# First layer: head norm's scale and shift folded to the queries, sums of squares moved, row maxima half a group ahead

## The reference

```python
q = (layernorm(x, ln_q_g, ln_q_b) @ Wq + bq).reshape(b, c, HEAD, HD)      # 16 heads of 16
k, v = ...                                                                # the same from Wkv
q, k = apply_rotary(q * scale, x), apply_rotary(k * scale, x)             # scaled by the norm of x's rows
qn, kn = layernorm(q, ln_h_g, ln_h_b), layernorm(k, ln_h_g, ln_h_b)       # over a head's 16 features
att = softmax(einsum(qn, kn) / sqrt(HD))                                  # 1024 queries x 1024 keys
a = einsum(att, v) @ Wo + bo
```

## Time and profile before

| | |
|---|---|
| median of three runs | 2325.57 us (2319.04 to 2331.56) |
| profiled execution | 2323.5 us, its span 2322.0 us |
| busy over the span | TensorE 2008.8, VectorE 1449.2, ScalarE 1252.5, POOL 876.0 us |
| projection, first normalisation to last evacuation | about 32 to 205 us |
| attention, first row score to last output | 205.3 to 629.3 us |
| granted TensorE clock, 61 to 70 us, 70 to 79 us | 0.51, 1.00 of 2.4 GHz |

### The profile page before, as it was taken

One profiled execution on the slowest core, in us unless ns is written; L12 is line 12 of the kernel. 1 busy time (PEld: TensorE's weight loads), 2 busy tenths in 40 slices (PEclk: granted clock), 3 DMA queues, 4 the chain that ended last, 5 costly groups with the idle time before them and its releaser, 6 DMA issues. The chain is left out here.

```text
span 2322.0 us, 41383 instructions
## 1 busy us (share of the span) xinstructions
PE 2008.8 (87%) x11710; PEld 1336.4 (58%) x11710; DVE 1449.2 (62%) x3073; ACT 1252.5 (54%) x2550; POOL 876.0 (38%) x899
## 2 busy tenths in 40 slices
PE   4886999999767769999738899999788999997698
PEld 1442233333144559999714577777544777775587
DVE  4776888888055669999447665665255555543443
ACT  0573577777733337777214477777144777771322
POOL 1221000000035547798153177777100666670100
PEclk7895799999977879999869999999898999998899
DMA  7953000000061148899421011212000011112000
GB/s 212 289 95 46 11 1 0 0 0 1 25 183 78 69 138 262 264 281 278 139 68 50 8 44 42 50 44 53 19 0 1 24 23 32 23 35 68 0 19 18
DMA packets 186850, 173.82 MB, mean 75 GB/s; under 512 B 20755, under 2 KB 171653, under 8 KB 185734
## 3 DMA queue, kind: packets, MB, share of 16 engines
q1 hardware_dynamic: 174662, 143.23, 22.3%
q0 software_dynamic: 10720, 29.44, 3.8%
q10 hardware_dynamic: 1376, 0.02, 0.0%
HBM read 96.15 MB, written 61.60 MB: 68 GB/s over the span
## 5 line engine op out<-in xcount | busy, mean ns | idle before, releaser
L2611 POOL TENSOR_TENSOR w_rest<-work,w_head 128x512 fp32r<-128x512 f32 (+3 forms) x384 | 395.3, 1042 | 223.5 <-ACT w_head L2568 221.1
L769 DVE TENSOR_REDUCE half_max<-m_ps 128x1 f32<-128x512 f32 x512 | 316.6, 682 | 53.7 <-PE m_ps L694 53.2
L2457 DVE TENSOR_REDUCE piece_max<-m_ps 128x1 f32<-128x512 f32 (+3 forms) x384 | 200.8, 548 | 203.4 <-PE m_ps L2384 159.9
L823 ACT ACTIVATE weights<-s_ps 128x512 f32<-128x512 f32 x512 | 266.4, 602 | 100.1 <-PE s_ps L709 100.1
L2564 ACT ACTIVATE work<-s_ps 128x512 f32<-128x512 f32 (+3 forms) x384 | 187.6, 488 | 100.9 <-PE s_ps L2412 96.0
L2568 ACT ACTIVATE w_head<-work 128x512 fp32r<-128x512 f32 (+3 forms) x384 | 201.4, 524 | 57.0 <-PE o_ps L2421 46.0
L694 PE MATMUL m_ps<-kT,qT 96*128 (+1 forms) x512 | 211.8, 416 | 6.5 <-DVE half_max L769 4.5
L709 PE MATMUL s_ps<-qT,kT 99*128 (+1 forms) x512 | 191.3, 386 | 7.3 <-ACT weights L823 7.3
L2421 PE MATMUL o_ps<-w_head,lat_head 128*128 128x512 f32 (+3 forms) x384 | 184.3, 480 | 1.6 <-POOL w_rest L2611 1.5
L859 POOL COPY v_now<-v 128x83 f32 (+1 forms) x64 | 16.1, 258 | 375.3 <-PE o_ps L721 370.0
L709 PEld LDWEIGHTS s_ps<-qT,kT 99*128 (+1 forms) x512 | 49.0, 98 | 160.7 <-ACT weights L823 66.8
(11 more groups left out here) (393 smaller groups left out, 5038.6 us busy)
## 6 DMA issues: line engine op xcount, KB each, us to landing
slots<-zero SPq DMA_DIRECT2D x8, 3456.0 KB, 27.4
rows<-slots SPq DMA_DIRECT2D x64, 256.0 KB, 3.4
slots<-ex_out SPq DMA_DIRECT2D x64, 256.0 KB, 3.0
ex_wgv<-in_L_ffn_wg_dram SPq DMA_DIRECT2D x72, 176.0 KB, 3.0
ex_wgv<-in_L_ffn_wv_dram SPq DMA_DIRECT2D x72, 176.0 KB, 3.2
ex_wo<-in_L_ffn_wo_dram SPq DMA_DIRECT2D x72, 128.0 KB, 3.1
oT<-work SPq DMA_DIRECT2D x64, 128.0 KB
w_down<-l_inverse SPq DMA_DIRECT2D x32, 256.0 KB
```

The source lines that it names most:

```text
L769: dve.tensor_reduce(half_max[:, u:u + 1], m_ps[:, BANK[u], :], AX.X, ALU.max).then_inc(max_done, 1)
L823: act.activation(w[:, s % 2 * 4 + j, :], s_ps[:, BANK[4 * s + j], :], ACT.Exp, scale=HD ** -0.5).then_inc(w_done, 1)
L2457: dve.tensor_reduce(piece_max[:, qt, k0 // 512:k0 // 512 + 1], m_ps[:, r % 2, 0:n], AX.X, ALU.max).then_inc(d["max_done"], 1)
L2611: pool.tensor_tensor(w_rest[:, s % 3, c0:512], w[:, s % 3, c0:512], w_head[:, s % 3, c0:512], ALU.subtract).then_inc(d["w_rest_done"], 1)
```

## The change

The product of the two normalised heads, (yq g + b)(yk g + b) summed over the features, differs from (yq g² + g b) yk only by terms that are the same for all keys of a query, and the softmax drops those. So the queries are multiplied by g² and g b is added, and the keys stay as they are: L441 and L444 act on half of the columns, and two small products at the start make g² and g b.

In the projection's steps VectorE sums the squares of tile t before it centres tile t+1 (`variance`), and ScalarE takes the deviation after the first two of the four evacuations, with the copy, the squares and the other two behind it.

In the attention the row scores are ordered by halves of the queries: the first 32 of a group belong to the first 512 queries of all four heads. The maxima are split, turned, copied and placed twice per group, each half for itself, and the lead is 11 steps (half a group and three) instead of 19. Four transposes of 12 columns take the place of one of 96, the copy is 12 x 512 instead of 96 x 128, and one transfer takes the place of three.

```diff
-        v_ones = m.sem("pr_v_ones")
+        v_ones, both_done = m.sem("pr_v_ones"), m.sem("pr_both_done")
...
+                dve.tensor_tensor(b_h[:, :], g_h[:, :], b_h[:, :], ALU.mult).then_inc(both_done, 1)
+                dve.wait_ge(both_done, 1)
+                dve.tensor_tensor(g_h[:, :], g_h[:, :], g_h[:, :], ALU.mult).then_inc(both_done, 1)
+                dve.wait_ge(both_done, 2)
...
-                def scale(t, u):
+                def variance(t, u):
 
                     dve.wait_ge(sq_done, t + 1)
                     dve.tensor_reduce(hvar[:, u, :], oth[:, u], AX.X, ALU.add).then_inc(sqs_done, 1)
+
+                def scale(t, u):
+
...
-                    dve.tensor_tensor(own[:, u], val[:, u], g_h[:, :].unsqueeze(1).to_broadcast([P, NH, HD]), ALU.mult
+                    dve.tensor_tensor(own[:, u, 0:H0, :], val[:, u, 0:H0, :],
+                                      g_h[:, :].unsqueeze(1).to_broadcast([P, H0, HD]), ALU.mult
                                       ).then_inc(unit_done, 1)
                     dve.wait_ge(unit_done, 2 * t + 2)
-                    dve.tensor_tensor(val[:, u], own[:, u], b_h[:, :].unsqueeze(1).to_broadcast([P, NH, HD]), ALU.add
+                    dve.tensor_tensor(val[:, u, 0:H0, :], own[:, u, 0:H0, :],
+                                      b_h[:, :].unsqueeze(1).to_broadcast([P, H0, HD]), ALU.add
                                       ).then_inc(val_done, 1)
 
                 def step(t, u, b):
                     more = not isinstance(t, int) or t + 1 < T
                     if more:
                         rotate_parts(t + 1, 1 - u, (t + 1) // TB if b is None else b)
+                    variance(t, u)
                     if more:
                         centre(t + 1, 1 - u)
                     scale(t, u)
...
-                        evacuate(before, t - 2, u)
+                        evacuate(before, t - 2, u, range(2))
+                    deviation(t, u)
                     if not isinstance(t, int) or t > 0:
                         more_parts(t - 1, 1 - u)
                     if more:
                         squares(t + 1, 1 - u)
-                    deviation(t, u)
+                    if not isinstance(t, int) or t > 1:
+                        evacuate(before, t - 2, u, range(2, 4))
...
-    LEAD = 3
+    HALF = NU // 2
+    LEAD = 8 + 3
...
-            return [(1 + more, u) if 1 + more <= left else None for more, u in ahead]
+            return [(more, u) if more <= left else None for more, u in ahead]
...
-                    j, qt, kh = u // 16, u // 2 % 8, u % 2
+                    j, qt, kh = u % HALF // 8, u // HALF * 4 + u // 2 % 4, u % 2
...
-                    pe.transpose(t_bf[0:QK0, 0:P], shift[:, :, :], c.identb[:, :]).then_inc(shT_done, 1)
+                    for q in range(4):
+                        i = pe.transpose(t_bf[0:SHIFT_ROWS, q * P:(q + 1) * P],
+                                         shift[:, q].rearrange("p i j -> p (i j)"), c.identb[:, :])
+                    i.then_inc(shT_done, 1)
...
-                    if u == 0:
-                        pe.wait_ge(placed, g * PLACED + PLACED)
+                    if kt == 0 and j == 0:
+                        pe.wait_ge(placed, g * 2 * PLACED + (qh + 1) * PLACED)
...
-                        turn_outputs(g, 0, False)
+                        turn_outputs(g, 0, True)
+                    if s == 5:
+                        turn_shift(g, 1)
                     if s == 13 and left:
-                        turn_shift(g + 1)
+                        turn_shift(g + 1, 0)
...
-                for u in range(NU):
+                for u in range(4 * LEAD):
+                    if u == HALF + 3:
+                        turn_shift(0, 0)
                     row_scores(0, u)
-                for u in range(4 * LEAD):
-                    if u == 3:
-                        turn_shift(0)
-                    row_scores(1, u)
...
+                    if s == 4:
+                        parts(g, 1)
                     if s == 12 and left:
-                        parts(g + 1)
+                        parts(g + 1, 0)
...
+                        if s == 6 and j == 0:
+                            copy_shift(g, 1)
                         if s == 14 and j == 0 and left:
-                            copy_shift(g + 1)
+                            copy_shift(g + 1, 0)
...
-                for g in range(NG):
-                    sp.wait_ge(sh_copied, g + 1)
-                    for part in range(3):
-                        row = QK0 + part
-                        sp.dma_start(q_g[row:row + 1, g, :, :].rearrange("o h (t n) -> o (h t) n", n=P),
-                                     shift_rows[32 * part:32 * part + 32, :]).then_inc(placed, 16)
+                for n in range(2 * NG):
+                    sp.wait_ge(sh_copied, n + 1)
+                    first = n % 2 * 512
+                    sp.dma_start(q_g[QK0:ROWS0, n // 2, :, first:first + 512], shift_rows[0:SHIFT_ROWS, :]
+                                 ).then_inc(placed, 16)
```

More of the change, by code:

```diff
@@ L524, in more_parts, with evacuate @@
                     act.activation(stack[:, u, :, 4 * HD:5 * HD], rest[:, :, :], ACT.Copy).then_inc(p2_done, 1)
-                def evacuate(b, t, u):
-                    for i in range(4):
+                def evacuate(b, t, u, banks=range(4)):
+                    for i in banks:
                         act.wait_ge(turned, t * 4 + (i + 1))
@@ L638, in l0_attend @@
         half_max = l.sb("half_max", [P, NU])
[L639 to L642, removed]
+        row_max = l.sb("row_max", [P, HALF // 2])
+        rest = l.sb("max_rest", [P, HALF // 2])
+        shift = l.sb("max_parts", [P, 4, 3, 4], BF16)
+        shift_rows = l.sb("max_rows", [P, 512], BF16)
+        by_tile = shift[:, :, :, :].rearrange("p q i j -> p i j q")
+        row_maxima, row_rests = (y[:, :].rearrange("p (j q) -> p j q", j=4) for y in (row_max, rest))
         v_now = l.sb("v_now", [P, TB, VG])
@@ L692, in row_scores, with turn_shift @@
                     if not (isinstance(g, int) and g == 0 and u < BACK[u]):
-                        pe.wait_ge(max_done, g * NU + (u - BACK[u] + 1))
+                        pe.wait_ge(max_done, g * NU + (FREE_M + u - BACK[u] + 1))
                     pe.matmul(m_ps[:, BANK[u], :], q_g[0:QK0, g, j, qt * P:(qt + 1) * P],
                               k_g[0:QK0, g, j, kh * 512:(kh + 1) * 512], start=True, stop=True).then_inc(m_done, 1)
[L697 to L700, removed]
-                    pe.transpose(t_bf[0:QK0, 0:P], shift[:, :, :], c.identb[:, :]).then_inc(shT_done, 1)
+                def turn_shift(g, qh):
+                    pe.wait_ge(parts_done, g * 2 + (qh + 1))
+                    if not (isinstance(g, int) and g == 0 and qh == 0):
+                        pe.wait_ge(att_done, g * 2 + (FREE_A + qh - 1))
+                    for q in range(4):
+                        i = pe.transpose(t_bf[0:SHIFT_ROWS, q * P:(q + 1) * P],
+                                         shift[:, q].rearrange("p i j -> p (i j)"), c.identb[:, :])
+                    i.then_inc(shT_done, 1)
                 def scores(g, s, j):
@@ L769, in maximum, with parts @@
                     dve.tensor_reduce(half_max[:, u:u + 1], m_ps[:, BANK[u], :], AX.X, ALU.max).then_inc(max_done, 1)
[L771 to L778, removed]
-                    dve.tensor_scalar(shift[:, 0, :], row_max[:, :], -1.0, None, ALU.mult).then_inc(neg_done, 1)
-                    dve.wait_ge(neg_done, g + 1)
-                    dve.scalar_tensor_tensor(rest[:, :], row_max[:, :], -1.0, shift[:, 0, :], ALU.mult,
+                def parts(g, qh):
+                    n = g * 2 + qh
+                    dve.wait_ge(max_done, n * HALF + (FREE_M + HALF))
+                    dve.tensor_reduce(row_max[:, :], half_max[:, qh * HALF:(qh + 1) * HALF].rearrange(
+                        "p (r h) -> p r h", h=2), AX.X, ALU.max).then_inc(comb_done, 1)
+                    dve.wait_ge(comb_done, n + 1)
+                    if not (isinstance(g, int) and g == 0 and qh == 0):
+                        dve.wait_ge(shT_done, n)
+                    dve.tensor_scalar(by_tile[:, 0], row_maxima, -1.0, None, ALU.mult).then_inc(neg_done, 1)
+                    dve.wait_ge(neg_done, n + 1)
+                    dve.scalar_tensor_tensor(row_rests, row_maxima, -1.0, by_tile[:, 0], ALU.mult,
                                              ALU.subtract).then_inc(r_done, 1)
-                    dve.wait_ge(r_done, g * 2 + 1)
-                    dve.tensor_copy(shift[:, 1, :], rest[:, :]).then_inc(r_done, 1)
-                    dve.wait_ge(r_done, g * 2 + 2)
-                    dve.tensor_tensor(shift[:, 2, :], rest[:, :], shift[:, 1, :], ALU.subtract).then_inc(parts_done, 1)
+                    dve.wait_ge(r_done, n * 2 + 1)
+                    dve.tensor_copy(by_tile[:, 1], row_rests).then_inc(r_done, 1)
+                    dve.wait_ge(r_done, n * 2 + 2)
```

(23 more changed lines are left out.)

7 lines of the change are left out of this document (4 added, 3 removed).

## The result

The changed kernel took 2295.34 us in the median of four runs (2291.65 to 2300.19) against 2328.57 for four of the kernel before: a ratio of 0.9863, with a 95% interval from 0.9823 to 0.9904. By the ratio that is about 32 us faster, where 24 were forecast, and inside the range of the prediction. The profiled execution took 2300.19 us (span 2298.7).

A forecast was written before the change was run, and what follows sets the result against it. TensorE paces the steady attention; in the projection no engine is full, a tile being a round trip. Terms +0.4 - 16.6 - 4.0 - 13.6 + 5.8 + 4.1 = -23.9 us, from 2325.57 to 2301; 80% range 2290 to 2314.

The forecast's parts named there:

- The set-up: Start of the projection: two small products ahead of the first normalisation cost 0.4 us (bounds 0.2 and 1.0).
- The tile: Projection: two VectorE waits vanish and two operations halve; a tile falls from 8.63 to 7.25 us, twelve save 16.6.
- The loop that I named: Projection tile: centring, squares, two evacuations, turned x, first part, POOL to next centring; 7.15 us by busy times, the limit that stays.
- Rival (1): Projection: VectorE and POOL block each other in full, 8.2 us per tile, twelve save only 5 us; 2313 us, chance 0.13.
- The tail: Last rotation to first row score: shorter queue ahead of the last deviation and shorter tiles save 4.0 us (2.6 to 5.5).
- The opening: First row score to first score: 45.94 us falls to 32.3, held by SP's duplications; 13.6 us saved (12.6 to 15.3).
- The groups: Attention: seven more transposes 0.43 us, second splitting 0.4 us per group; seven groups lose 5.8 us (3.0 to 10.2).
- Rival (2): Attention groups: the second splitting holds TensorE in full, costing 17.3 us instead of 5.8; 2313 us, chance 0.13.
- The end: Last eight attention steps that had no row scores: 32 row scores reappear there, 4.1 us lost.
- The new waits: Attention: ninth-step score waits for its half's transfer, which arrives over 2 us early; turning first-half outputs costs nothing.
- (3): Projection: its change does nothing as another wait replaces those removed; 2322 us, chance 0.08.
- (4): Projection: TensorE's granted clock stays at 1.2 GHz through all twelve tiles, 37.8 us come back; 2339 us, chance 0.06.

The follow-up runs named there:

- e4: The changed kernel with scale and shift on queries and keys again and without the two small products at the start; 2302.15 us in one execution.
- e9: The changed kernel with POOL's two subtractions for the third part on one head each instead of sixteen; 2287.85 us in one execution.
- e1: The changed kernel with the first half group's maxima sent from ScalarE's queue instead of SP's; 2283.36 us, 0.982 of the kernel before.
- e8: The changed kernel with VectorE doing the splitting of the maxima twice each time, into unread tiles; 2312.48 us in one execution.
- e2: Only the projection's part of the change, with the attention of the kernel before; 2292.80 us in one execution.
- e11: e10 with the splitting behind the row maxima moved to POOL, VectorE keeping only the reduction; 2282.17 us, 0.982 of the kernel before.
- e7: The changed kernel with the four transposes of the split maxima issued twice each time; 2294.72 us in one execution.
- e5: The changed kernel with ScalarE's old order (four evacuations, copy, squares, deviation), early sum and fold kept; 2308.15 us in one execution.
- e10: e1 with the two small products made behind the first three normalisations; 2288.73 us, 0.9848 of the kernel before.

## Why the prediction was right

**The set-up.** The first normalisation comes 0.78 us later: 0.43 for the two products (forecast 0.4) and 0.35 that were there ahead of them.

**The tile.** The steps held in the main: both waits went, the fold shortened VectorE's chain (e4), and the next limit is a loop through ScalarE's first part and POOL's rest, with TensorE beside it. Two parts of the working were off. The loop that I named, through ScalarE's queue, was added up from busy times (7.15 us); by starts its operations overlap, and e9 shows it at 6.90. And it is not quite the longest. VectorE alone was taken for 6.46 us, but halved operations take 0.42 us and not 0.35, and L403 is stretched by 0.36, so that VectorE's own operations from the sum to `val`, and not ScalarE's queue, close the loop at 6.95: ScalarE's first part starts 0.03 us after `val` is written. That is why lengthening them in e4 costs its 0.53 us in full. That the two lie 0.05 us apart is luck. The size came out as 7.02 us on average instead of 7.25, so 19.4 us instead of 16.6, 1 to 2 of them from that one execution. I had also put POOL's stretch on the centring. It fell on the normalisation and on POOL itself. The reading of it before was loose too: at 68.39 us L426 had used up its extra 0.33 us at 68.72, while L475 ran until 68.88, so the two met, but the stretch cannot be read as ending with L475. Rival (1), 8.2 us per tile, is refuted.

**The tail.** 4.8 us instead of 4.0; the queue ahead of the last deviation was halved as said, and VectorE's wait for it fell from 4.60 us to 2.24:

```profile
166.98 0.35 DVE L445 RECIPROCAL hstd<-hstd 128x32 f32<-128x32 f32 x1 [2.24 <-ACT hstd L526]
```

**The opening.** 31.93 us where 32.3 was taken, for the reason given: e1 takes SP's queue away and the opening falls to the 27.0 us worked out without it.

**The groups.** 0.69 us per group instead of 0.83: 0.39 for the transposes (forecast 0.43) and the 0.30 left for the splitting (forecast 0.4). The argument for it, that row scores wait only after a step's slack is used, holds for this splitting, and e8 shows that it would have been wrong for one more. Rival (2) needed 2 x 1.02 us in full and is refuted.

**The end.** 7.9 - 7 x 0.69 = 3.1 us against 4.1, by subtraction; runs with the same attention differ by up to 1.7 us in this stretch, so no miss is shown.

**The new waits** cost nothing: no half's first score waits for its transfer in the steady groups.

**Rivals (3) and (4)** did not come. The projection gained most of the whole (e2), and in the changed kernel, through the twelve tiles the granted clock was full, in this view of busy times by stretch (the engines in the order TensorE, its weight loads, VectorE, ScalarE, POOL; then clock and transfers):

```profile
73.39:157.63 84.24, 82.53 (x562) 48.61 (x563) 78.53 (x144) 75.44 (x121) 35.67 (x36) 1.00 0.83 207
```

The stages gained 6 us more than the sum has: 2.8 in the twelve tiles, 2.0 because the groups and the end cost less than taken, 0.8 in the tail, and the rest in the opening and in a tile for which the sum has no term. The median time fell further still, but the totals of single executions spread by more than this.

## What to carry to other kernels

Where several engines hand a tile round and none is full, look for the operation that waits in an engine's queue behind work that nobody needs yet; moving it pays only when its own input is moved ahead too. When a lead is shortened, ask which transfer the waiting step depends on and what stands ahead of it in its queue: here a transfer of 12 KB behind 128 KB ones took back 5 us, and issuing it from an idle engine gave them back. The slack of an engine beside the bound hid most of the first added microsecond here and nothing of the second, so neither its idle share nor a run with the work doubled gives the price of what was added: doubling prices the next piece, and the piece itself is priced by taking it away, as e11 does for both splittings together.

## What the runs showed of the hardware

The first tiles do not run alike from execution to execution of the same instructions. The granted clock of TensorE from 40 to 46 us, in the same view as above, in the changed kernel and in e7, which differs from it only in the attention, and once more for e7 from 70 us:

```profile
40.00:46.00 6.00, 5.13 (x10) 2.46 (x10) 1.96 (x4) 0.38 (x1) 0.00 (x0) 0.50 1.02 290
```

```profile
40.00:46.00 6.00, 4.88 (x15) 1.99 (x14) 3.42 (x6) 1.28 (x3) 0.00 (x0) 1.00 1.03 290
...
70.00:76.00 6.00, 6.00 (x36) 3.95 (x35) 4.90 (x9) 5.39 (x9) 2.85 (x3) 0.82 1.03 288
```

TensorE had been at work in both (busy for 5.49 of the 6 us before), and one was granted 1.2 GHz, the other 2.4. The fourth rotation starts at 73.39 us in the one and 68.87 in the other: 4.5 us without any change in the projection. Part of that is lost again: e7's next tile still has the lower clock in part and takes 8.50 us instead of 7.64, and at the last rotation e7 is 3.2 us ahead (154.44 against 157.63). Six more runs, e1, e5, e8, e9, e10 and e11, were early like e7: their third rotation starts between 57.78 and 59.13 us, that of the changed kernel at 64.74. The stages behind the attention took between 1686.9 us (e2) and 1701.3 (after) on the same code. What decides either stays open; both are as large as some of the effects above, which is why those are read from stages and not from totals.
